# Layer normalisation, token and channel diffusion and routed experts: the product with Wo in float32r pieces loaded by groups, and ScalarE in the second normalisation

## The reference, cut to what matters

```python
xn = layernorm(x)                                       # first normalisation
# token diffusion, 16 heads of 16 features
z = layernorm(xn, ln1_w, ln1_b)
qk, v = heads(z @ Wqk_t), heads(z @ Wv_t)
logits = (2 * qk @ qk.T - q2[:, None] - q2[None, :]) / sqrt(16) * tau_t
o = merge(softmax(logits) @ v)
x1 = xn + (o @ Wo_t) * gamma1                           # the product with Wo
# channel diffusion, 8 heads of 32 channels
a2 = layernorm(x1, ln2_w, ln2_b)                        # second normalisation
p = softmax(channel_logits(a2.T @ a2, Wqk_c) * tau_c)
x2 = x1 + (a2 @ Wv_c @ p.T @ Wo_c) * gamma2
# one of eight experts for each token, chosen by a router
y = gate * (relu(xn @ W1[e] + b1[e]) @ W2[e] + b2[e])
out = x + x2 + y
```

## Time and profile before

| what | value |
|---|---|
| median of 3 runs | 1295.04 us (1294.8 to 1295.06) |
| the profiled execution | 1294.12 us, of which its span (first to last instruction) is 1292.4 |
| TensorE busy | 1262.2 us, 98% of the span |
| ScalarE busy | 1042.0 us, 81% |
| VectorE busy | 459.4 us, 36% |
| GpSimd busy | 216.1 us, 17% |
| granted TensorE clock, mean | 0.999 of full |

### The profile page before, as it was taken

The page is one execution under the profiler, slowest core; times in us unless marked ns, Lnnn a source line. Parts: engine busy times, 40 slices in busy tenths (PEclk is TensorE's granted clock), DMA queues, the critical chain, the costliest instruction groups (busy, mean ns, idle before and its releaser), DMA issues. The chain is left out here.

```text
span 1292.4 us, 42497 instructions
## 1 busy us (share of the span) xinstructions
PE 1262.2 (98%) x18323; PEld 726.1 (56%) x18323; DVE 459.4 (36%) x1229; ACT 1042.0 (81%) x1180; POOL 216.1 (17%) x310
## 2 busy tenths in 40 slices
PE   8989999999999999999999999999999999999988
PEld 6544334555555555555555555555555555555877
DVE  6964001232222223222223223222222322225867
ACT  6779999888888888888888888888888888884120
POOL 3212441111101011111111111100111111102860
PEclk9999999999999999999999999999999999999999
DMA  6598446665474564665574456556456556633673
GB/s 196 200 280 217 105 94 201 147 170 127 146 161 115 154 149 112 168 153 122 133 187 123 130 122 186 124 158 148 110 143 166 122 138 183 166 110 119 142 134 127
DMA packets 161460, 193.46 MB, mean 150 GB/s; under 512 B 64152, under 2 KB 128664, under 8 KB 157816
## 3 DMA queue, kind: packets, MB, share of 16 engines
q1 hardware_dynamic: 148008, 168.83, 49.4%
q0 software_dynamic: 13264, 21.90, 7.1%
HBM read 154.63 MB, written 35.95 MB: 147 GB/s over the span
## 5 line engine op out<-in xcount | busy, mean ns | idle before, releaser
L962 ACT ACTIVATE shared<-ps 128x1024 f32<-128x1024 f32 x1024 | 968.9, 1042 | 120.3 <-PE ps L1106 120.0
L1129 PE MATMUL ps<-shared,work 128*17 128x256 f32 x7680 | 475.9, 379 | 0.0
L1106 PE MATMUL ps<-mov,stat 52*128 52x512 f32 x2048 | 345.1, 433 | 10.2 <-ACT shared L962 9.7
L985 DVE TENSOR_TENSOR work<-ps,work 128x256 f32<-128x256 f32 x258 | 109.6, 425 | 563.9 <-PE ps L1151 561.7
L1129 PEld LDWEIGHTS ps<-shared,work 128*17 128x17 f32 x7680 | 219.4, 98 | 149.2 <-issue 24.3
L1106 PEld LDWEIGHTS ps<-mov,stat 52*128 52x128 f32 x2048 | 166.8, 185 | 195.6 <-issue 104.8
L1142 PE MATMUL ps<-XNW,work 128*32 128x256 f32 x2496 | 196.1, 390 | 0.0
L1151 PE MATMUL ps<-work,XNW 128*32 128x128 f32 x4992 | 190.9, 273 | 0.5 <-DVE work L973 0.5
L1151 PEld LDWEIGHTS ps<-work,XNW 128*32 128x32 f32 x4992 | 148.8, 110 | 51.5 <-DMA early<-in_L_ffn_b_dram 0.7
L810 POOL DMA_DIRECT2D y_slots<-work x39 | 22.0, 564 | 552.7 <-DVE work L991 505.1
L1142 PEld LDWEIGHTS ps<-XNW,work 128*32 128x32 f32 x2496 | 51.7, 108 | 106.6 <-issue 99.9
(11 more groups left out here) (168 smaller groups left out, 643.3 us busy)
## 6 DMA issues: line engine op xcount, KB each, us to landing
XNW<-in_L_ffn_W_dram SPq DMA_DIRECT2D x78, 1024.0 KB, 6.2
stat<-q_parts SPq DMA_DIRECT2D x192, 128.0 KB
mov<-q_parts SPq DMA_DIRECT2D x192, 64.0 KB
q_parts<-XNW SPq DMA_DIRECT2D x16, 512.0 KB, 5.0
x_slots<-work SPq DMA_DIRECT2D x1, 4992.0 KB, 17.5
early<-x_slots SPq DMA_DIRECT2D x156, 32.0 KB, 2.2
early<-in_L_ffn_b_dram SPq DMA_DIRECT2D x39, 128.0 KB, 8.2
y_slots<-work POOLq DMA_DIRECT2D x39, 128.0 KB, 2.2
```

Source lines behind the costliest of these rows:

```text
L962: nc.scalar.activation(probs[:, q % DEEP], ps[:, at:at + 2].rearrange("p a b -> p (a b)"), ACT.Exp, scale=head_scale).then_inc(probs_ready, 1)
L985: ins = nc.vector.tensor_tensor(ysb[:, slot], ps[:, EX, 0:D], ysb[:, slot], ALU.add)
L1106: last = nc.tensor.matmul(ps[:, at + r], stat[rows, head % 2, m * P:(m + 1) * P], mov[rows, head % 2, half * 512:(half + 1) * 512], start= ...
L1129: last = nc.tensor.matmul(ps[32 * j:32 * j + VW, AV, half * 256:(half + 1) * 256], Vh[:, head % 2, m], probs[:, q % DEEP, j * 256:(j + 1) ...
```

## The change

The product with Wo changes from float32 to float32r. Each operand is split into an upper piece (the value as float32r holds it) and the rest, and three of the four products of pieces are added up: upper x upper, upper x rest, rest x upper, two matmuls (KC) each. Wo is split once, in late constants on VectorE. The attention output is split head by head in `norm_o`: a wide copy and a wide subtract follow the transposition, and `store_o` writes both pieces, in eight transfers. AT becomes four slots of one group each, with both pieces; `load_at(G)` loads one group in two transfers of 512 KB. Groups 0 to 3 are loaded in block one (now only when all V has been copied, since the slots cover all of V's place), groups 4 to 7 in block two when their slot's project is done.

In the second normalisation, GpSimd's rstd makes two more small operations (the product of mean and rstd, and its negative, `nmr`), ScalarE's new `make_z2` centres and scales the rows into a2g in four activations, and VectorE's make_a2 is left with two wide operations a group, times ln2_w and plus ln2_b.

```diff
 norm_o (VectorE, once a head)
-            at_least(nc.vector, o_stored, 16 * NCHUNK * head)
-            nc.vector.transpose(o_cols, o_rows).then_inc(o_ready, 1)
+            nc.vector.transpose(o_cols, o_rows).then_inc(o_flipped, 1)
+            nc.vector.wait_ge(o_flipped, head + 1)
+            at_least(nc.vector, o_stored, O_DMAS * 16 * head)
+            nc.vector.tensor_copy(o_parts[:, 0].bitcast(F32R), o_cols).then_inc(o_upper, 1)
+            nc.vector.wait_ge(o_upper, head + 1)
+            nc.vector.tensor_tensor(o_parts[:, 1].bitcast(F32R), o_cols, o_parts[:, 0], ALU.subtract).then_inc(o_ready, 1)
 store_o (GpSimd) and load_at (SyncE)
-                nc.gpsimd.dma_start(rows[j], o_cols[32 * j:32 * j + DH].rearrange("d (k n) -> d k n", k=2)
-                                    ).then_inc(o_stored, 16)
+                for part in range(2):
+                    rows = a_turned[part, head * DH:(head + 1) * DH].rearrange("d (k j n) -> j d k n", k=2, j=NCHUNK)
+                    nc.gpsimd.dma_start(rows[j], o_parts[32 * j:32 * j + DH, part].rearrange("d (k n) -> d k n", k=2)
+                                        ).then_inc(o_stored, 16)
+        def load_at(G):
+            b, at = G // GB, (G % GB) * GN
+            for part in range(2):
+                nc.sync.dma_start(AT_raw[:, G % AT_SLOTS, part], a_turned[part, b * D:(b + 1) * D, at:at + GN]
+                                  .rearrange("(c p) n -> p c n", p=P)).then_inc(at_loaded[G % AT_SLOTS], 16)
 late constants (VectorE, once)
+                    mark(nc.vector.tensor_copy(wo_parts[:, 0], wo[:, :, :]))
+                    mark(nc.vector.tensor_tensor(wo_parts[:, 1], wo[:, :, :], wo_up, ALU.subtract))
 SyncE, block two
+                for G in range(GB, GROUPS):
+                    sp.wait_ge(wo_ready, 2 * (G - AT_SLOTS) + 2)
+                    load_at(G)
 rstd (GpSimd)
-                    nc.gpsimd.tensor_tensor(rs1[:, par], ve1[:, par], nhalf[:, 0], ALU.pow).then_inc(rstd3_ready, 1)
+                    nc.gpsimd.tensor_tensor(rs1[:, par], ve1[:, par], nhalf[:, 0], ALU.pow).then_inc(rs1_step, 1)
+                    pool.wait_ge(rs1_step, 2 * G + 1)
+                    nc.gpsimd.tensor_tensor(nmr[:, par], mv1[:, par, :, 0], rs1[:, par], ALU.mult).then_inc(rs1_step, 1)
+                    pool.wait_ge(rs1_step, 2 * G + 2)
+                    nc.gpsimd.tensor_scalar(nmr[:, par], nmr[:, par], -1.0, None, ALU.mult).then_inc(rstd3_ready, 1)
 ScalarE
+                def make_z2(G, par):
+                    act.wait_ge(rstd3_ready, G + 1)
+                    at_least(act, gram_done, G - 1)
+                    if G >= 2:
+                        act.wait_ge(ring3_ready, use_a2(G - 2) + KC)
+                    for t in range(GT):
+                        last = nc.scalar.activation(a2g[:, par, t], XN[:, G * GT + t], ACT.Identity,
+                                                    bias=nmr[:, par, t:t + 1], scale=rs1[:, par, t:t + 1])
+                    last.then_inc(z2_ready, 1)
+                make_z2(0, 0)
+                make_z2(1, 1)
                 for G in range(GB):
                     take_a2(G, G % 2)
+                    make_z2(G + 2, G % 2)
                 take_gram(0)
...
                 take_a2(GROUPS - 4, 0)
+                make_z2(GROUPS - 2, 0)
                 take_a2(GROUPS - 3, 1)
                 exp_of(0)
+                make_z2(GROUPS - 1, 1)
                 take_a2(GROUPS - 2, 0)
                 take_r(0)
 make_a2 (VectorE)
-                    for t in range(GT):
-                        last = nc.vector.scalar_tensor_tensor(a2g[:, par, t], tile(XN, G, t), mv1[:, par, t, 0:1],
-                                                              l2w[:, :], ALU.subtract, ALU.mult)
...
-                    for t in range(GT):
-                        last = nc.vector.scalar_tensor_tensor(a2g[:, par, t], a2g[:, par, t], rs1[:, par, t:t + 1],
-                                                              l2b[:, :], ALU.mult, ALU.add)
+                    dve.wait_ge(z2_ready, G + 1)
+                    nc.vector.tensor_tensor(a2g[:, par], a2g[:, par], l2w[:, :].unsqueeze(1).broadcast_to([P, GT, D]),
+                                            ALU.mult).then_inc(a2_step, 1)
+                    nc.vector.tensor_tensor(a2g[:, par], a2g[:, par], l2b[:, :].unsqueeze(1).broadcast_to([P, GT, D]),
+                                            ALU.add).then_inc(a2_ready, 1)
 project (TensorE)
-                                last = nc.tensor.matmul(ps[:, 2 + k, t * D:(t + 1) * D], AT[:, b, c, cols], wo[:, c],
-                                                        start=(c == 0), stop=(c == KC - 1))
+                            terms = [(a, w, c) for a, w in ((0, 0), (0, 1), (1, 0)) for c in range(KC)]
+                            for n, (a, w, c) in enumerate(terms):
+                                last = nc.tensor.matmul(ps[:, 2 + k, t * D:(t + 1) * D], AT[:, slot, a, c, cols],
+                                                        wo_parts[:, w, c], start=(n == 0), stop=(n == len(terms) - 1))
```

More of the change, by code:

```diff
@@ L99, in build @@
         VR = D + NE
+        V_at = nc.sbuf_base
         Vflat = sb("V", [P, NB * TB * VR])
@@ L136, in build @@
         bv_heads = bv[:, :].rearrange("p (h d) -> p h d", h=H)
+        xg_at = nc.sbuf_base
         xg = sb("xg", [P, 2, GT, D])
+        wo_parts = nc.alloc_sbuf_tensor_at("wo_parts", [P, 2, KC, D], F32R, offset=xg_at)
+        wo_up = wo_parts[:, 0].bitcast(F32)
         mid = ctx.enter_context(ExitStack())
@@ L199, in build @@
         wr = take_b([GN])
+        o_parts = big[:, 2 * S - 2 * 512:].rearrange("p (k n) -> p k n", k=2)
         spare = take([3 * GN])
@@ L751, in build @@
         o_ready = sem("o_ready")
+        o_flipped = sem("o_flipped")
+        o_upper = sem("o_upper")
+        O_DMAS = 2 * NCHUNK
         o_stored = sem("o_stored")
@@ L796, in build @@
         xn_back = [sem(f"xn_back{k}") for k in range(3)]
-        at_loaded = [sem("at_loaded0"), sem("at_loaded1")]
+        at_loaded = [sem(f"at_loaded{k}") for k in range(AT_SLOTS)]
         HOMES = ((0, 1, 6, 7), (2, 3), (4, 5))
@@ L802, in store_o @@
             nc.gpsimd.wait_ge(o_ready, head + 1)
-            rows = a_turned[head * DH:(head + 1) * DH].rearrange("d (k j n) -> j d k n", k=2, j=NCHUNK)
             for j in range(NCHUNK):
-                nc.gpsimd.dma_start(rows[j], o_cols[32 * j:32 * j + DH].rearrange("d (k n) -> d k n", k=2)
-                                    ).then_inc(o_stored, 16)
+                for part in range(2):
[7 more added lines that the diff above has]
+                                  .rearrange("(c p) n -> p c n", p=P)).then_inc(at_loaded[G % AT_SLOTS], 16)
         def store_y(n):
@@ L904, in _ @@
                         n += 1
-                sp.wait_ge(o_stored, 16 * NCHUNK * H)
-                sp.wait_ge(v_copied, H)
-                sp.dma_start(AT[:, 0], a_turned[0:D].rearrange("(c p) n -> p c n", p=P)).then_inc(at_loaded[0], 16)
+                sp.wait_ge(o_stored, O_DMAS * 16 * H)
+                sp.wait_ge(v_copied, NB * H)
+                for G in range(GB):
+                    load_at(G)
                 load_xn(0)
@@ L1254, in build @@
         a2_ready = sem("a2_ready")
+        z2_ready = sem("z2_ready")
+        rs1_step = sem("rs1_step")
         expert_added = sem("expert_added")
@@ L1286, in _ @@
                 load_xn(2)
-                sp.wait_ge(o_stored, 16 * NCHUNK * NB * H)
-                sp.wait_ge(v_copied, NB * H)
-                for j in range(NCHUNK):
-                    at = slice(j * 512, (j + 1) * 512)
-                    sp.dma_start(AT[:, 1, :, at], a_turned[D:2 * D, at].rearrange("(c p) n -> p c n", p=P)
-                                 ).then_inc(at_loaded[1], 16)
+                sp.wait_ge(o_stored, O_DMAS * 16 * NB * H)
+                for G in range(GB, GROUPS):
+                    sp.wait_ge(wo_ready, 2 * (G - AT_SLOTS) + 2)
+                    load_at(G)
                 for G in range(GROUPS):
@@ L1520, in project @@
                 def project(G, par):
-                    b, at = G // GB, (G % GB) * GN
-                    pe.wait_ge(at_loaded[b], 16 if b == 0 else 16 * NCHUNK)
+                    slot = G % AT_SLOTS
+                    pe.wait_ge(at_loaded[slot], 2 * 16 * (G // AT_SLOTS + 1))
                     for k in range(2):
@@ L1525, in project @@
                         for t in range(2):
-                            cols = slice(at + (2 * k + t) * P, at + (2 * k + t + 1) * P)
-                            for c in range(KC):
-                                last = nc.tensor.matmul(ps[:, 2 + k, t * D:(t + 1) * D], AT[:, b, c, cols], wo[:, c],
-                                                        start=(c == 0), stop=(c == KC - 1))
+                            cols = slice((2 * k + t) * P, (2 * k + t + 1) * P)
```

(4 more changed lines are left out.)

12 lines of the change are left out of this document (4 added, 8 removed).

## The result

| what | before | after |
|---|---|---|
| median of 4 runs each, us | 1294.92 (1293.81 to 1295.06) | 1310.72 (1310.06 to 1311.37) |
| ratio, 95% interval | | 1.0119 (1.0104 to 1.0133) |
| the profiled execution, and its span | 1294.12, 1292.4 | 1311.37, 1309.5 |
| TensorE busy | 1262.2 us | 1265.7 us (97% of the span) |
| granted TensorE clock, mean | 0.999 | 0.990 |

The change makes the kernel 1.2% slower, about 15.8 us by the medians. The forecast was 1308.8 us, with a range of 1302 to 1317. In the code after the change, the lines that matter are L858 and L860 (the split in norm_o), L1326, L1328 and L1330 (rstd and its two additions), L1367 (make_z2), L1375 and L1377 (take_gram), L1358 (take_a2), L1389 (take_r), L1566 (project), L1592 (corner), L1599 (product_t), L1584 (gram_of), L1627 (product_r), L1636 (product_m) and L1458 (make_a2).

What follows compares the result with a forecast made beforehand. TensorE bounds the kernel before, where GpSimd's lateness costs nothing. Terms 9.3 + 1.6 - 0.4 + 2.5 + 0.8 = +13.8 us on the profiled 1294.12, plus 0.92 to the median: 1308.8 us, range 1302 to 1317.

Steps and rivals of the forecast that it cites:

- rival C: End of batch 0: ScalarE is not held and TensorE stays the bound; faster, 1291.6 us; chance 0.04.
- rival D: End of batch 0: ScalarE not held, projections at 3.0 us, slow clock stretch kept; about as before, 1295 us; chance 0.03.
- step 2: Last head: the uncovered split and eight stores instead of four start GpSimd's rstd(0) later, +1.6 us.
- step 3: GpSimd's rstd: two small operations add 0.6 us a group, +3.6 us by the end of rstd(5).
- step 4: ScalarE's make_z2(5) waits for GpSimd ahead of take_gram(0), delaying the product with Wqk and gram_of(4), +9.3 us.
- step 5: TensorE's clock: the new rest after project(6) brings one slow stretch, +1.6 us.
- step 6: Float32r projections take 3.0 us, saving 0.45 a group; only project(7), behind the stall, counts: -0.4 us.
- step 8: End of batch 0: make_z2(7) ahead of take_a2(6) and take_r(0) costs +2.5 us, plus 0.8 for a possible slow stretch.
- Step 1: The split in norm_o, 1.46 us a head, is hidden beside TensorE's attention work; charged 0, upper end 0.3 us.
- rival B: Attention pays for the split at its 28 head boundaries, 9 us: 1318 us; chance 0.06.
- Rival A: GpSimd's additions in rstd are dear, by their price or waiting for VectorE: +11.9, 1321 us; chance 0.13.
- Step 7: make_a2 on VectorE shrinks by some 0.9 us a group, but VectorE waits for z2 anyway; charged 0.

Runs made afterwards that it cites:

- experiment 3: Changed kernel with make_z2(5) moved behind take_t(0) and make_z2(7) behind take_r(0) in ScalarE's order: 1304.26 us.
- experiment 4: Changed kernel with two more 128x4 multiplications by 1.0 on GpSimd in each rstd: 1315.55 us.
- experiment 1: Changed kernel with the old second normalisation, so only the product with Wo is new: 1295.0 us, ratio 0.9989 to the kernel before.
- experiment 6: Changed kernel with GpSimd's list reordered, rstd(G) two groups ahead of its own group's gathers (rstd(7) only one): 1307.47 us.
- experiment 7: Changed kernel with make_z2(5) and make_z2(7) moved later on ScalarE and rstd ahead of the gathers on GpSimd: 1303.87 us.
- experiment 8: Kernel before with ten unused 128x128 matmuls added on TensorE where the attention begins: 1294.08 us, ratio 0.9995.
- experiment 10: Kernel before with the product with Wo in pieces, the old second normalisation, and ten unused matmuls at the attention's start: 1294.63 us, ratio 0.9994.
- experiment 5: Changed kernel with make_z2(7) alone moved behind take_r(0) on ScalarE: 1309.36 us.
- Experiment 9: Changed kernel with ten unused 128x128 matmuls on TensorE at the attention's start: 1308.31 us.

## Why the prediction was right

The mechanism was right: ScalarE waits for GpSimd at make_z2(5), and TensorE for ScalarE. Moving that wait away took 6.5 us off (experiment 3), and lengthening GpSimd's list put 4.8 on (experiment 4); rivals C and D fall with the 8.17 us of rest. Step by step, from the two profiled executions, all less the 2.98 us by which the whole tail starts later (the last head's last transposition at 1186.43, at 1183.45 in the earlier trace rows):

| place | forecast, us later | measured |
|---|---|---|
| rstd(0) starts (step 2) | 1.6 | 1.22 |
| nmr(5) ready (step 3) | 5.2 | 4.57 |
| product_t(0) starts (step 4) | 9.3 | 8.73 |
| gram_of(4) starts (step 5) | 10.9 | 10.51 |
| rstd(7) starts (step 6) | 10.5 | 10.29 |
| gram_of(7) starts (step 8) | 13.8 | 14.12 |
| end of the program | 13.8 | 14.1 |

The mechanism is right at each place; that the end comes out within 0.3 is partly luck, since the way to product_t(0) was 0.6 cheaper than forecast and step 8 0.5 dearer.

- *Step 1.* In the profile of after the split is hidden, as forecast, and rival B falls with it: from the first turn_o to the last head's last transposition it is 1060.31 us, where the kernel before took 1060.38. At the head boundary of the earlier trace rows, which stands at 738 us in after, VectorE's and TensorE's timeline reads:

```profile
737.47 0.43 DVE L858 CAST work<-work 128x512 fp32r<-128x512 f32 x1
...
737.93 0.69 DVE L860 TENSOR_TENSOR work<-work 128x512 fp32r<-128x512 f32 x1
738.54 0.42 DVE L1008 TENSOR_TENSOR work<-ps,work 128x256 f32<-128x256 f32 x1
...
738.87 0.34 DVE L1014 TENSOR_SCALAR work<-ps,work 128x128 f32<-128x128 f32 x1
...
739.43 0.64 PE L1167 MATMUL ps<-XNW,work 128*32 128x256 f32 x8
```

  Copy and subtract end at 738.62, the takings at 739.21, and TensorE starts at 739.43. Of 1.43 us of cover 0.22 is left. A second edit of that size would not be free. The forecast's own sign, an attention longer by more than a microsecond, does appear in four other profiles with the split (experiments 1, 3, 6 and 7, 1.2 to 2.3 us longer). It does not come from the head boundaries: in each of the four TensorE rests once, for 1.4 to 2.2 us near 362 us, and the distance from one head's end to the next is as before for the other heads, to 0.4 us. In experiment 3 the row is

```profile
363.68 0.52 PE L1176 MATMUL ps<-work,XNW 128*32 128x128 f32 x10 [2.23 <-issue]
```

  The profile shows nothing that this rest waits for. Experiment 4 has one of 0.60 us, and neither the other four kernels with the split nor the three without it have one; its cause stays open.
- *Step 2* was 0.4 too dear, 0.3 of it because the copy took 0.43 us and not 0.69: I had priced both operations by a row with two operands. The Trainium skill states on the page Advanced Engine Details and Errata, section VectorE Performance Modes, that a copy or cast from SBUF to SBUF can run at two elements a cycle; the trace points the same way, 427 ns for the cast beside 692 for the subtract of the same size, a factor of 1.6.
- *Step 3.* The two small operations took 0.20 and 0.24 us, with their waits about 0.6 in all, as forecast. Rival A falls. The prediction had also weighed the Trainium skill's rule of the exclusive lock (SBUF — State Buffer, its section on the two separate sides), by which the sum would have been 1317. In after it does not show: the means are 200 and 239 ns, and the pow's is 1064, under that of the earlier trace rows. There the wide operations begin only when z2, and so rstd, is done, and GpSimd is by then in its gathers. Where the order puts the two side by side, in experiment 6, the trace agrees with the rule: 1.26 us for 0.20.
- *Steps 4 and 5.* As forecast, also one slow stretch: product_t(0) is 1.79 us longer.
- *Step 6.* A projection takes 3.11 us in its row and 2.95 from its start to the next line's, against 3.0; only the one behind the stall counted. In experiment 1, where no stall swallows the others, product_t(0) comes 40.29 us behind the last transposition, against 42.16 before: 1.87 for the four projections ahead of it. By its ratio the whole gained 1.4 us (0 to 2.7).
- *Step 7* was an oversight that cost nothing here and became the bound in experiment 3. Before, VectorE could subtract the mean while rstd was still to come; now everything waits for it. The pow with its two operations (1.65 us), z2 (2.07) and two wide operations (2 x 1.23) are 6.2 us in a row where before the pow and four operations of 0.48 were about 3. In after the stall covers that. In the third experiment it is the last part of what gram_of(6) and gram_of(7) wait for; for gram_of(6) GpSimd's list stands ahead of it, since rstd(6) starts there only at 1242.16, with no rest before it.
- *Step 8.* 3.83 us against 2.5 and half of 1.6. The slow stretch did fall there (product_m(0) took 3.62 us), but it is no sign of this step: product_m(0) also took 3.78, 3.60 and 3.78 us in the profiles of experiments 1, 8 and 10, which have the old normalisation and whose longest rest at the place is as the kernel before has it (2.1 to 2.3 us). And the place has two limits, and the prediction named only the order; undoing that alone (experiment 5) gave nearly nothing, since a2(7) was as late.
- *Step 9.* The loads were hidden, as forecast: no project in after waits for one.
- *The term that is missing* is the 3 us at the attention's start: 10.24 us at half clock, no part of the change in the code. Experiment 9 took it out. It would have been no fault of a step if it came by chance alone. In the profiles without the ten matmuls all seven kernels with the new second normalisation have such a stretch, and the two without it have none. Whether that is chance stays open; I see no path by which code that runs 1100 us later could act there, and the two traces agree to 0.03 us up to the start of the logits on which the clock falls, with the same rest ahead of them. Before, then after:

```profile
92.16 0.49 PE L1106 MATMUL ps<-mov,stat 52*128 52x512 f32 x2 [1.44 <-ACT shared L962]
```

```profile
92.19 0.80 PE L1131 MATMUL ps<-mov,stat 52*128 52x512 f32 x2 [1.43 <-ACT shared L985]
```

  Whether the kernel before has the stretch in other executions is not shown. Its mean clock was 0.995 to 0.997 in 13 of 17 runs, and 0.999 in its profile, but experiments 1 and 10 have a mean of 0.996 in their profiles with no slow stretch at the attention's start.

The measured median lies 1.9 us above the forecast, and these 3 us at the attention's start are more than that.

## What to carry to other kernels

Before work is moved to an engine that is mostly idle, look at what stands behind it in that engine's list and at who is late ahead of it: ScalarE was busy for only 16 of the 42.6 us from 1195.40 on and was still made late, because its new work waited for the one engine that had no rest. Ask of each moved operation also what it can no longer overlap with: the old normalisation did half its work before rstd was there, the new one does none. And when an order is undone and little comes back, look for the second limit at the same place before giving up the first.

## What the runs showed of the hardware

- TensorE's granted clock fell to 0.50 in the attention's first microseconds, where TensorE rests 0.4 to 1.4 us at a time between its first logits, in 7 of 9 profiles, for 3.4 to 10.2 us; with ten small matmuls in the gaps it did so in none of 3, but only one of these three kernels had shown the fall without them. The rests alone do not decide it: the kernel before has the same ones and kept its clock. At its longest the fall delayed the kernel by 3 us.
- Behind rests of 2.1 to 2.3 us at the end of batch 0 product_m(0) ran in 1.99 us in the kernel before, and in 3.60 to 3.78 in experiments 1, 8 and 10: the same place, at either level of the clock.
- 24 float32r matmuls of 256 columns took 2.95 us, 0.123 each. The float32 product that they replace took 0.216 for each of its two passes, 0.43 together.
- A 128x4 operation on GpSimd took 0.20 us by itself and 1.26 beside a wide operation of VectorE with two inputs.
